# A recommender tower on one core: rows stored chunk by chunk, half loads in long runs, and GpSimd's index add moved to the head of its chunk

## The chip, the cores and the metric

The kernel runs on one core of a Trainium2 chip. The time is the device time of one execution in microseconds. Before the change it was 2475.34 us, the median of three runs from 2474.52 to 2476.03.

## The reference, cut to what matters

39 embedding tables are read at 2048 x 39 ids (rows of D = 16 floats). Three layers then each form all products of a field of the input with a field of the layer before, weigh them with W and sum, per sample b and embedding position d. A small dense part of two hidden layers ends it.

```python
e = stack([tbl_f[ids[:, f]] for f in range(39)], axis=1)        # (2048, 39, 16)
x0 = xk = e
for idx, (W, b) in enumerate([(w0, b0), (w1, b1), (w2, b2)]):
    z = relu(einsum('bhd,bkd,hks->bsd', x0, xk, W) + b[None, :, None])
    if idx != 2:
        xk = z[:, :64, :];  direct.append(z[:, 64:, :])
    else:
        direct.append(z)
logit = sum(concatenate(direct, axis=1), axis=-1)                # (2048, 256)
h = concatenate([logit, dense_ctx], axis=1)
h = maximum(h @ W_top1 + b_top1, 0);  h = maximum(h @ W_top2 + b_top2, 0)
y = h @ W_top3
```

All of it is float32. W is (39, 39, 128) in layer 0 and (39, 64, 128) in layers 1 and 2.

## The kernel before, in words

The 2048 samples are done in 64 chunks of CB = 32, so a tile's free size is CN = 32 x 16 = 512. A chunk c has three stages, one per layer, and every engine does them in the order stage 1 of c, stage 0 of c + 1, stage 2 of c.

**Rows.** GpSimd gathers a chunk's rows three chunks ahead: it adds each table's first row to the ids (`index`, L417) and issues ten indirect DMAs (L429) into `rows_sb[p]`, p being the chunk's parity. SP stores these rows transposed to a DRAM tensor `x0_rows` (L336, six DMAs of 64-byte pieces). `x0_rows` has one line of all 2048 samples per field (58 lines, fields 0 to 18 a second time after the 39), so a chunk's piece of a field is 2 KB and neighbouring fields of a chunk lie 128 KB apart. From it the operands are loaded:

- `xa`, `xb` (L346, L350): for stage 0, three blocks of 39 partitions each, the fields and the shifted fields, all issued by SP.
- `xh[p]` (L304): for stages 1 and 2, every field spread over 64 partitions. Tile t holds field 2t in partitions 0 to 63 (SP's DMA) and field 2t + 1 in partitions 64 to 127 (ScalarE's DMA). There are 20 tiles and 39 fields; the last tile's upper half is cleared at the start (`pads_cleared`), by a memset of GpSimd for each of the two buffers.

**Products.** VectorE multiplies two tiles at once, 128 x 1024 (L516). A pair (a "group") has one of three kinds. WHOLE goes to TensorE as float32. The other two are split in a rounded high part, made by ScalarE (L775), and the rest, the low part, made by GpSimd (L458, BY_POOL) or by VectorE (L490, BY_DVE). A split tile takes three fast matmuls, a whole tile two slow ones of two passes each (L627). Per chunk GpSimd makes ten low parts: four in stage 1, two in stage 0, four in stage 2. In a chunk that gathers, one indirect DMA follows each low part; chunk 0 issues twenty, for chunks 2 and 3, and chunks 61 to 63 issue none.

**What sets the order around the change.** Each engine has its own instruction stream, written out by hand in the blocks `sync`, `gpsimd`, `vector`, `tensor`, `scalar`; the engines meet at semaphores. Chunks 0 and 1 and the last two (four on GpSimd) are written out, the others are a loop of two chunks a turn, with waits on register values. In GpSimd's `chunk`, `begin_gather` comes after the chunk's first low part: it waits for the ids, adds, waits for `stored[p]` (the rows buffer is free once the chunk before in it is stored) and for its own add. SP's `chunk(c)` stores the rows of c, fetches the ids of c + 2, waits for its stores, loads `xa` and `xb`, then the lower half of `xh`, and stores the sums of chunk c - 2. ScalarE issues the upper half of chunk c + 1 at the head of its chunk c. After the 64 chunks the dense part runs, in buffers that are free by then.

Of the kernel before, what the change touches and what calls it, by code (L numbers as in the profile page):

```python
# [44 lines left out]
G0, GK = -(-T0 // PAIR), TK // PAIR  # L45
# [3 lines left out]
KINDS = {  # L49
    0: [BY_POOL, BY_DVE, BY_POOL, WHOLE],  # L50
    1: [WHOLE, BY_POOL, WHOLE, BY_DVE, BY_POOL, WHOLE, BY_POOL, BY_DVE, BY_POOL, WHOLE],
}
KINDS[2] = KINDS[1]
# [18 lines left out]
class Group:  # L72


    def __init__(self, stage, chunk, g, counts):
        total = T0 if stage == 0 else TK
        self.stage, self.chunk, self.g, self.kind = stage, chunk, g, KINDS[stage][g]
        self.tiles = range(PAIR * g, min(PAIR * (g + 1), total))
        self.ends_layer = self.tiles[-1] == total - 1
        self.rows = 128 if stage else (LAST0 if self.ends_layer else JT * F)  # L80
# [11 lines left out]
def plan():  # L92


    counts = dict.fromkeys(("all", "split", WHOLE, BY_POOL, BY_DVE), 0)
    order = [(0, 0)]
    for c in range(CHUNKS):
        order += [(1, c)] + [(0, c + 1)] * (c + 1 < CHUNKS) + [(2, c)]
    return {(stage, c): [Group(stage, c, g, counts) for g in range(len(KINDS[stage]))]
            for stage, c in order}  # L100
# [5 lines left out]
WHOLES = [g for g in EVERY if not g.split]  # L106
LIKE = 2

PER = {"all": sum(map(len, KINDS.values())),
       "split": sum(k != WHOLE for ks in KINDS.values() for k in ks),  # L110
       BY_POOL: sum(k == BY_POOL for ks in KINDS.values() for k in ks),
       BY_DVE: sum(k == BY_DVE for ks in KINDS.values() for k in ks)}
assert (PER["all"] - PER["split"]) % WHOLE_SLOTS == 0
assert PER[BY_POOL] % POOL_SLOTS == 0 and PER["split"] % SPLIT_SLOTS == 0
# [10 lines left out]
def tower(nc, table, ids, row_base, ctx_t, staged, wt1, wt1c, wt2, cols, out):  # L125
# [3 lines left out]
    x0_dram = nc.dram_tensor("x0_rows", (XROWS, N), f32, kind="Internal").ap()  # L129
    feats_dram = nc.dram_tensor("feats_all", (128, 2, B), f32, kind="Internal").ap()  # L130

    with ExitStack() as stack:
# [60 lines left out]

        def split_places(weights, products):
# [16 lines left out]
        wt2_end = -(-(3 * T1 + n1 * T2) // S)  # L211
        WT2_FREE = 1 + max(g.n for g in PLAN[2, CHUNKS - 1]
                           if g.split and SPLIT_TILE[2, g.tiles[0]] < wt2_end)
        INPUTS_FREE = 1 + max(g.n for g in SPLITS if g.split_slot < 2)
# [17 lines left out]
        pads_cleared = sem("pads_cleared")  # L232
# [33 lines left out]
        def groups(stage, c):  # L266

            return PLAN[stage, c if isinstance(c, int) else LIKE + (stage == 0)]

        def count(c, group, value, per):  # L270


            if isinstance(c, int):
                return value
            return (c - group.chunk) * PER[per] + value
# [10 lines left out]
        def over_chunks(engine, step, tail=2):  # L286

            step(0, 0)
            step(1, 1)
            with engine.Fori(1, (CHUNKS - tail) // 2) as i:  # L290
                step(2 * i, 0)
                step(2 * i + 1, 1)
            for c in range(CHUNKS - tail, CHUNKS):
                step(c, c % 2)
# [12 lines left out]
        N_GROUPS, N_SPLIT = len(firsts), sum(g.split for g in firsts)  # L307
# [11 lines left out]
        def _(sp):  # L319
            def load_ids(c, p):  # L320
                sp.dma_start(ids_sb[p][:, :], ids[bass.ds(c * 128, 128), :]).then_inc(ids_loaded[p], 16)

            def store_rows(c, p):

                sp.wait_ge(gathered[p], 8 * GATHERS * (c - p) + 16 * GATHERS)
                col = x0_dram[:, bass.ds(c * CN, CN)]
                for again in range(2):
                    for g in range(FG):  # L330
                        f0 = g * GATHERS
                        n = min(GATHERS, (XROWS - F if again else F) - f0)
                        if n > 0:
                            src = rows_sb[p][g * CB:(g + 1) * CB, 0:n * D]
                            dst = col[again * F + f0:again * F + f0 + n, :]
                            sp.dma_start(dst.rearrange("f (b d) -> b f d", d=D),  # L336
                                         src.rearrange("b (f d) -> b f d", d=D)
                                         ).then_inc(stored[p], 16)

            def load_pairs(c):  # L340

                col = x0_dram[:, bass.ds(c * CN, CN)]
                for jj in range(JT):
                    n = (SHIFTS - jj + JT - 1) // JT
                    at = slice(jj * F, (jj + 1) * F)
                    sp.dma_start(xa[at, :], col[0:F, :]).then_inc(x0_loaded, 16)  # L346
                    step = col.ap[0][0]
                    shifted = bass.AP(tensor=col.tensor, offset=col.offset + jj * step,
                                      ap=[[step, F], [JT * step, n], [1, CN]])
                    sp.dma_start(xb[at, 0:n, :], shifted).then_inc(x0_loaded, 16)  # L350

            def store_feats(c, p):

                sp.wait_ge(direct_summed, c + 1)
                sp.wait_ge(last_summed, c + 1)
# [56 lines left out]
        def _(pool):  # L412
# [65 lines left out]
            for g in groups(0, 0):  # L478
                if g.kind == BY_POOL:
                    low_parts(g, 0)  # L480
# [461 lines left out]
```

## Time and profile before

| what | value |
|---|---|
| profiled execution's own time | 2474.38 us |
| its span | 2472.6 us |
| TensorE busy | 2373.9 us, 96% |
| VectorE busy | 2212.4 us, 89% |
| GpSimd busy | 2155.9 us, 87% |
| ScalarE busy | 1364.1 us, 55% |
| DMA moved | 467 MB, 189 GB/s over the span |

Busy is the sum of an engine's instructions; matmuls overlap and their ends are modelled, so TensorE's share is not its share of peak. Register instructions and the issue of plain DMAs are not counted as busy; an indirect DMA on GpSimd is. An engine's idle time is put down to the semaphore that ended it, or to "issue" when nothing that the profile shows was waited for.

### The profile page before, as it was taken

The page shows a single profiled execution, that of the slowest core. Times are in us where ns is not written, and L with a number is a line of the kernel's source. Part 1 is how long each engine was busy: PE and PEld are TensorE (multiplying, and loading weights), DVE is VectorE, ACT ScalarE, POOL GpSimd, SP SyncE. Part 2 cuts the span into 40 slices and gives each one's busy share as a digit, 9 for nine tenths or more (in the row PEclk, how much of TensorE's full clock was granted, in tenths as well). Part 3 has the DMA queues.
Part 4 walks back from the last instruction along what each step waited for, and adds up shares of the span by engine and source line. Part 5 has one row for each costly group of instructions (what it writes and reads, how often), then busy time and mean ns, then how long its engine had stood idle before and what let it go on. Part 6 is the DMA issues. An engine that isn't in the chain of part 4 may idle for free. (4 is left out here: it accounts for less than half of the span.)

```text
span 2472.6 us, 32417 instructions
## 1 busy us (share of the span) xinstructions
PE 2373.9 (96%) x8192; PEld 1539.6 (62%) x8192; DVE 2212.4 (89%) x2047; ACT 1364.1 (55%) x1532; POOL 2155.9 (87%) x1350
## 2 busy tenths in 40 slices
PE   1799999999999999999999999999999999999999
PEld 1466666666666666666666666666666666666665
DVE  2689999999999999999999999999999999999983
ACT  2355555555555555555555555555555555555552
POOL 4799999999999999999999999999999999999640
PEclk9899999999999999999999999999999999999999
DMA  7888888888878888888888788888888878888710
GB/s 179 187 187 207 196 185 211 212 173 209 207 186 194 210 209 176 204 211 181 203 204 209 177 204 212 181 206 205 201 180 208 214 177 208 208 188 191 199 55 1
DMA packets 398547, 467.04 MB, mean 189 GB/s; under 512 B 170337, under 2 KB 179553, under 8 KB 398257
## 3 DMA queue, kind: packets, MB, share of 16 engines
q1 hardware_dynamic: 299202, 302.30, 54.3%
q10 hardware_dynamic: 78848, 159.39, 24.7%
q0 software_dynamic: 20480, 5.15, 1.8%
q8 instruction: 8, 0.13, 0.0%
q14 instruction: 9, 0.07, 0.0%
HBM read 457.03 MB, written 9.71 MB: 189 GB/s over the span
## 5 line engine op out<-in xcount | busy, mean ns | idle before, releaser
L458 POOL TENSOR_TENSOR low<-prod_pool,high 128x1024 fp32r<-128x1024 f32 (+1 forms) x640 | 1532.5, 2395 | 88.8 <-ACT high L775 73.2
L775 ACT ACTIVATE high<-prod_pool 128x1024 fp32r<-128x1024 f32 (+1 forms) x640 | 677.3, 1058 | 733.5 <-DVE prod_pool L516 695.9
L627 PE MATMUL z<-prod_whole,w_whole 128*128 128x512 f32 (+1 forms) x2176 | 1011.5, 594 | 5.6 <-DVE prod_whole L516 5.6
L627 PE MATMUL z<-high,w_high 128*128 128x512 f32 (+1 forms) x1920 | 939.5, 489 | 55.9 <-ACT high L775 55.9
L627 PE MATMUL z<-high,w_low 128*128 128x512 f32 (+1 forms) x1920 | 758.6, 395 | 0.0
L429 POOL DMA_INDIRECT rows<-table,index x640 | 611.5, 955 | 147.8 <-issue 99.0
L516 DVE TENSOR_TENSOR prod_whole<-xh,x 128x1024 f32<-128x1024 f32 x512 | 620.5, 1212 | 110.1 <-PE z L627 90.8
L627 PE MATMUL z<-low,w_high 128*128 128x512 f32 (+1 forms) x1920 | 614.0, 401 | 33.5 <-POOL low L458 33.3
L627 PEld LDWEIGHTS z<-prod_whole,w_whole 128*128 128x128 f32 (+1 forms) x2176 | 412.7, 190 | 355.7 <-issue 296.8
L516 DVE TENSOR_TENSOR prod_pool<-xh,x 128x1024 f32<-128x1024 f32 x512 | 621.3, 1213 | 10.0 <-POOL low L458 10.0
L627 PEld LDWEIGHTS z<-high,w_high 128*128 128x128 f32 (+1 forms) x1920 | 363.6, 189 | 229.2 <-issue 141.1
L627 PEld LDWEIGHTS z<-high,w_low 128*128 128x128 f32 (+1 forms) x1920 | 363.8, 189 | 172.4 <-issue 107.5
L627 PEld LDWEIGHTS z<-low,w_high 128*128 128x128 f32 (+1 forms) x1920 | 356.3, 189 | 145.2 <-POOL low L458 66.3
L775 ACT ACTIVATE high<-prod_dve 128x1024 fp32r<-128x1024 f32 (+1 forms) x320 | 328.5, 1026 | 170.2 <-DVE prod_dve L516 154.9
L490 DVE TENSOR_TENSOR low<-prod_dve,high 128x1024 fp32r<-128x1024 f32 (+1 forms) x320 | 391.3, 1223 | 3.3
L516 DVE TENSOR_TENSOR prod_dve<-xh,x 128x1024 f32<-128x1024 f32 x256 | 312.8, 1222 | 0.0
L516 DVE TENSOR_TENSOR prod_pool<-xb,xa_ps 117x1024 f32<-117x1024 f32 x128 | 155.6, 1215 | 79.6 <-POOL low L458 40.6
L752 ACT ACTIVATE x<-z,cols_sb 64x512 f32<-64x512 f32 x256 | 166.6, 651 | 63.0 <-PE z L627 44.5
L757 ACT ACTIVATE direct<-z,cols_sb 64x512 f32<-64x512 f32 x128 | 87.5, 684 | 33.9 <-DVE chunk_feats L528 32.3
L516 DVE TENSOR_TENSOR prod_dve<-xb,xa_ps 117x1024 f32<-117x1024 f32 x64 | 78.2, 1221 | 0.0
L765 ACT ACTIVATE xa_ps<-xa 117x512 f32<-117x512 f32 x64 | 38.6, 603 | 43.0 <-DMA xb<-x_rows 41.5
L742 ACT ACTIVATE last<-z,cols_sb 128x512 f32<-128x512 f32 x64 | 42.7, 668 | 4.9 <-PE z L627 4.9
(45 smaller groups left out, 365.5 us busy)
## 6 DMA issues: line engine op xcount, KB each, us to landing
xh<-x_rows SPq DMA_DIRECT2D x64, 2560.0 KB, 16.5
xh<-x_rows ACTq DMA_DIRECT2D x64, 2432.0 KB, 20.6
xb<-x_rows SPq DMA_DIRECT2D x128, 546.0 KB
xb<-x_rows SPq DMA_DIRECT2D x64, 468.0 KB
xa<-x_rows SPq DMA_DIRECT2D x192, 78.0 KB
rows<-table,index POOLq DMA_INDIRECT x640
x_rows<-rows SPq DMA_DIRECT2D x256, 20.0 KB
xh<-staged SPq DMA_DIRECT2D x2, 1280.0 KB, 6.9
```

Of the source, the lines that this page charges most:

```text
L429: pool.indirect_dma_start(rows_sb[p][0:n, j * D:(j + 1) * D], None, table, bass.IndirectOffsetOnAxis(ap=index[p][0:n, j:j + 1], axis=0),). ...
L458: pool.tensor_tensor(low[0:g.rows, g.split_slot, 0:n, :], prod_pool[0:g.rows, g.slot, 0:n, :], high[0:g.rows, g.split_slot, 0:n, :].bitcas ...
L490: dve.tensor_tensor(low[0:g.rows, g.split_slot, 0:n, :], prod_dve_v[0:g.rows, 0:n, :], high[0:g.rows, g.split_slot, 0:n, :].bitcast(f32), ...
L516: dve.tensor_tensor(into[0:g.rows, 0:n, :], spread[0:g.rows, t, :], shared[0:g.rows, :].unsqueeze(1).broadcast_to([g.rows, n, CN]), ALU.mu ...
L627: return pe.matmul(z[stage][:, :], weights[0:g.rows, table[stage, t], :], src[0:g.rows, i, :], start=t == 0 and weights is not w_low and s ...
L742: act.activation(last[:, :], z[2][:, :], ACT.Relu, bias=bias[2]).then_inc(relu_done[2], 1)
L752: act.activation(xk[stage][half, :], z[stage][feed, :], ACT.Relu, bias=bias[stage][feed, :]).then_inc(relu_done[stage], 1)
L757: act.activation(direct[leave, :], z[stage][leave, :], ACT.Relu, bias=bias[stage][leave, :]).then_inc(relu_done[stage], 1)
L765: act.activation(xa_ps[0:JT * F, :], xa[:, :], ACT.Copy).then_inc(xa_copied, 1)
L775: act.activation(high[0:g.rows, g.split_slot, 0:n, :], src[0:g.rows, 0:n, :], ACT.Copy).then_inc(high_ready, 1)
```

## The change

The order of fields in memory, the packets of the `xh` loads and the place of one small instruction change.

- `x0_rows` becomes (64 x 58) lines of 512, a chunk's 58 fields one after the other (`rows_of`).
- Tile t of `xh` holds fields t and 20 + t. The lower half of a chunk is one run of 40 KB per partition, the upper half one of 38 KB (`load_run`), cut by `max_dma_last_dim`. The last tile's upper half gets field 19 again, by a third DMA, and its weights are zero (`by_fields`), so the two memsets and `pads_cleared` go.
- GpSimd's `begin_gather` is parted. `make_index` (both waits and the add) comes ahead of the chunk's first low part, `begin_gather` keeps the wait for the add. In chunk 0 this holds for the first of its two gathers.
- In the dense part the split parts of the context lie in the weights' buffers instead of the products', and h1's two places further front.
- A class `Chunk` carries a chunk's number and parity, and the list of groups names each group's first tile; the groups are the same.

GpSimd's stream, in the loop, from the last gather of a chunk to the first of the next. `low` are the low parts, `rows` the gathered rows. Before:

```order
L458 TENSOR_TENSOR low<-prod_pool,high 128x1024 [waits high_ready]
L429 DMA rows1<-table,index1 96x16
L279 ISA
L458 TENSOR_TENSOR low<-prod_pool,high 128x1024 [waits high_ready]
L416 ISA
L417 TENSOR_TENSOR index0<-ids0,row_base_sb 128x10 [waits ids_loaded0]
L421 REGISTER_ALU
L422 REGISTER_ALU [waits stored0]
L429 DMA rows0<-table,index0 128x16 [waits index_ready]
```

The same place in the changed kernel:

```order
L481 TENSOR_TENSOR low<-prod_pool,high 128x1024 [waits high_ready]
L451 DMA rows1<-table,index1 96x16
L436 ISA
L439 REGISTER_ALU [waits ids_loaded0]
L440 TENSOR_TENSOR index0<-ids0,row_base_sb 128x10 [waits stored0]
L303 REGISTER_ALU
L481 TENSOR_TENSOR low<-prod_pool,high 128x1024 [waits high_ready]
L444 REGISTER_ALU
L451 DMA rows0<-table,index0 128x16 [waits index_ready]
```

The add and its two waits moved from behind the chunk's first low part to ahead of it; the gather's wait for the add stayed where it was.

SP's stream, in the loop, the loads of one chunk. Before:

```order
L279 ISA [waits stored0]
L346 DMA xa<-x0_rows 39x512 [waits products_ready]
L350 DMA xb<-x0_rows 39x7x512
L350 DMA xb<-x0_rows 39x6x512
L279 REGISTER_ALU
L304 DMA xh0<-x0_rows 64x20x512 [waits products_ready]
```

In the changed kernel:

```order
L303 ISA [waits stored0]
L371 DMA xa<-x0_rows 39x512 [waits products_ready]
L374 DMA xb<-x0_rows 39x7x512
L374 DMA xb<-x0_rows 39x6x512
L303 REGISTER_ALU
L330 DMA xh0<-x0_rows 64x5x2048 [waits products_ready]
L330 ISA
L330 DMA xh0<-x0_rows 64x512
```

SP's one load of twenty runs of 512 floats per partition became one of five runs of 2048 and a short one. ScalarE's load at the same place went from 19 runs of 512 to 8 runs of 1216 floats.

The diff, cut to its core (the many lines where only `c, p` became `c` are left out):

```diff
+RUN_BYTES = 4 * CN * 4
+HALF_TILE = TK - 1
...
-    x0_dram = nc.dram_tensor("x0_rows", (XROWS, N), f32, kind="Internal").ap()
+    x0_dram = nc.dram_tensor("x0_rows", (CHUNKS * XROWS, CN), f32, kind="Internal").ap()
...
-                    "feats": [x[:, 0:2, :], x[:, 3:5, :]],
-                    "ctx": [x[0:CTX, 2, :], x[0:CTX, 5, :]],
-                    "h1": x[:, 6:6 + n1, :]}
+                    "feats": [x[:, 0:2, :], x[:, 2:4, :]],
+                    "ctx": [w[0:CTX, CTX_AT:CTX_AT + MB], w[0:CTX, CTX_AT + MB:CTX_AT + 2 * MB]],
+                    "h1": x[:, 4:4 + n1, :]}
...
-        def load_fields(engine, c, p, hh):
-
-            col = x0_dram[:, bass.ds(c * CN, CN)]
-            step = col.ap[0][0]
-            n = (F + 1 - hh) // 2
-            spread = bass.AP(tensor=col.tensor, offset=col.offset + hh * step,
-                             ap=[[0, H], [2 * step, n], [1, CN]])
-            engine.dma_start(xh[p][hh * H:(hh + 1) * H, 0:n, :], spread).then_inc(xh_loaded[p], 16)
+        def rows_of(c):
+
+            return x0_dram[bass.ds(c.n * XROWS, XROWS), :]
+
+        def load_run(engine, c, part, tiles, field):
+
+            of = rows_of(c)
+            n = len(tiles)
+            spread = bass.AP(tensor=of.tensor, offset=of.offset + field * CN,
+                             ap=[[0, H], [1, n * CN]])
+            into = xh[c.p][part * H:(part + 1) * H, tiles[0]:tiles[0] + n, :]
+            engine.dma_start(into.rearrange("p t n -> p (t n)"), spread,
+                             max_dma_last_dim=RUN_BYTES).then_inc(xh_loaded[c.p], 16)
...
-                load_fields(sp, c, p, 0)
+                load_run(sp, c, 0, range(0, TK), 0)
+                load_run(sp, c, 1, range(HALF_TILE, TK), HALF_TILE)
...
-            def begin_gather(c, p):
-
-
-                pool.wait_ge(ids_loaded[p], 8 * (c - p) + 16)
-                pool.tensor_tensor(index[p][:, :], ids_sb[p][:, :], row_base_sb[:, :],
+            def make_index(c):
+                pool.wait_ge(ids_loaded[c.p], 8 * (c.n - c.p) + 16)
+                if not c.known or c.n >= 2:
+
+                    pool.wait_ge(stored[c.p], 8 * STORES * (c.n - c.p))
+                pool.tensor_tensor(index[c.p][:, :], ids_sb[c.p][:, :], row_base_sb[:, :],
                                    ALU.add).then_inc(index_ready, 1)
-                if not isinstance(c, int) or c >= 2:
-
-                    pool.wait_ge(stored[p], 8 * STORES * (c - p))
-                pool.wait_ge(index_ready, c + 1)
+
+            def begin_gather(c):
+                pool.wait_ge(index_ready, c.n + 1)
...
+                if ahead:
+                    make_index(ahead[0])
                 for i, (g, at) in enumerate(mine):
                     low_parts(g, at)
                     for _ in range(-(-len(left) // (len(mine) - i))):
-                        at, q, j = left.pop(0)
+                        at, j = left.pop(0)
                         if j == 0:
-                            begin_gather(at, q)
-                        gather(q, j)
+                            if at is not ahead[0]:
+                                make_index(at)
+                            begin_gather(at)
+                        gather(at.p, j)
...
-                dve.wait_ge(xh_loaded[p], 16 * (c - p) + 32)
+                dve.wait_ge(xh_loaded[c.p], 24 * (c.n - c.p) + 48)
...
-                load_fields(act, c, p, 1)
+                load_run(act, c, 1, range(0, HALF_TILE), TK)
...
-        tiles = np.zeros((2 * TK, H, w.shape[2]), w.dtype)
-        tiles[:F] = w
-        return np.ascontiguousarray(tiles.reshape(TK, 2 * H, w.shape[2]).transpose(1, 0, 2))
+        upper = np.concatenate([w[TK:], np.zeros_like(w[HALF_TILE:TK])])
+        return np.ascontiguousarray(np.concatenate([w[:TK], upper], axis=1).transpose(1, 0, 2))
```

## Rows read from the trace of the kernel before

**Rows 1.** The page's head.

```profile
span 2472.6 us, 32417 instructions
```

**Rows 2.** By stretch: busy of PE, PEld, DVE, ACT, POOL; clock; DMA share; GB/s.

```profile
1300.00:1600.00 300.00, 296.80 (x1029) 193.13 (x1028) 282.34 (x259) 173.51 (x192) 279.31 (x175) 1.00 0.85 196
```

**Rows 3.** Waits of PE, 100 to 2400 us: us in total, times, longest.

```profile
PE z L627 <- POOL low L458: 29.2, 64, 1.7
```

**Rows 4.** Timeline of PE: start, us, operation [idle before <-releaser].

```profile
1225.76 0.72 PE L627 MATMUL z<-low,w_high 117*128 117x512 f32 x2 [0.37 <-POOL low L458]
```

**Rows 5.** Groups on POOL, 200 to 2200 us: busy, mean ns | idle before.

```profile
L458 POOL TENSOR_TENSOR low<-prod_pool,high 128x1024 fp32r<-128x1024 f32 (+1 forms) x553 | 1324.7, 2396 | 14.9 <-ACT high L775 0.7
L429 POOL DMA_INDIRECT rows<-table,index x553 | 528.3, 955 | 123.9 <-issue 79.3 <-POOL index L417 44.6
```

**Rows 6.** Waits of POOL, 200 to 2200 us.

```profile
POOL rows L429 <- POOL index L417: 44.6, 55, 0.8
POOL low L458 <- ACT high L775: 0.7, 4, 0.2
```

**Rows 7.** Timeline of POOL over a chunk's edge.

```profile
1237.43 2.41 POOL L458 TENSOR_TENSOR low<-prod_pool,high 128x1024 fp32r<-128x1024 f32 x1
1239.99 0.92 POOL L429 DMA_INDIRECT rows<-table,index  x1 [0.16 <-issue]
1241.05 2.36 POOL L458 TENSOR_TENSOR low<-prod_pool,high 128x1024 fp32r<-128x1024 f32 x1
1243.38 0.21 POOL L417 TENSOR_TENSOR index<-ids,row_base_sb 128x10 int32<-128x10 int32 x1
1244.40 0.97 POOL L429 DMA_INDIRECT rows<-table,index  x1 [0.82 <-POOL index L417]
1245.39 2.40 POOL L458 TENSOR_TENSOR low<-prod_pool,high 128x1024 fp32r<-128x1024 f32 x1
```

**Rows 8.** Timeline of POOL at the start, before any low part.

```profile
15.78 0.92 POOL L429 DMA_INDIRECT rows<-table,index  x1 [0.30 <-issue]
16.73 0.29 POOL L417 TENSOR_TENSOR index<-ids,row_base_sb 128x10 int32<-128x10 int32 x1
```

**Rows 9.** Timeline of POOL in the last chunks, which gather nothing.

```profile
2312.19 2.38 POOL L458 TENSOR_TENSOR low<-prod_pool,high 128x1024 fp32r<-128x1024 f32 x1 [3.80 <-ACT high L775]
...
2347.62 2.37 POOL L458 TENSOR_TENSOR low<-prod_pool,high 128x1024 fp32r<-128x1024 f32 x1 [3.25 <-ACT high L775]
```

**Rows 10.** Timeline of SP, one chunk.

```profile
1216.79 2.98 SPq L336 DMA_DIRECT2D x_rows<-rows  x6
1219.99 1.22 SPq L321 DMA_DIRECT2D ids<-ids  x1
1223.67 0.35 SPq L346 DMA_DIRECT2D xa<-x_rows  x1
```

**Rows 11.** Timeline of ACT in chunks 0 and 1.

```profile
44.83 0.60 ACT L765 ACTIVATE xa_ps<-xa 117x512 f32<-117x512 f32 x1 [28.20 <-DMA xb<-x_rows]
...
83.44 0.60 ACT L765 ACTIVATE xa_ps<-xa 117x512 f32<-117x512 f32 x1 [13.31 <-DMA xb<-x_rows]
```

**Rows 12.** Timeline of PE in chunk 0.

```profile
85.07 0.79 PE L627 MATMUL z<-high,w_high 128*128 128x512 f32 x1 [7.89 <-ACT high L775]
```

**Rows 13.** By stretch: chunk 0's loads; the pairs' loads alone.

```profile
22.00:44.80 22.80, 0.00 (x0) 0.00 (x0) 0.00 (x0) 0.00 (x0) 6.71 (x8) 1.00 1.02 201
...
1223.00:1236.00 13.00, 12.63 (x44) 7.94 (x43) 12.83 (x12) 7.28 (x9) 12.45 (x8) 1.00 0.73 144
```

**Rows 14.** The page's DMA issues: KB each, median us to landing.

```profile
xh<-x_rows ACTq DMA_DIRECT2D x64, 2432.0 KB, 20.6
xb<-x_rows SPq DMA_DIRECT2D x128, 546.0 KB
xb<-x_rows SPq DMA_DIRECT2D x64, 468.0 KB
xa<-x_rows SPq DMA_DIRECT2D x192, 78.0 KB
```

**Rows 15.** DMA queues (q1 SP, q10 ACT), 1208 to 1214 us: packets, MB, share.

```profile
q1 hardware_dynamic: 541, 1.11, 52.5%
q10 hardware_dynamic: 532, 1.09, 51.5%
```

More of the change, by code:

```diff
@@ L75, in __init__ @@
     def __init__(self, stage, chunk, g, counts):
[L76 to L80, printed above, removed]
+        of = GROUPS[stage]
+        self.stage, self.chunk, self.g = stage, chunk, g
+        self.kind, first, n = of[g]
+        self.tiles = range(first, first + n)
+        self.begins_layer, self.ends_layer = g == 0, g == len(of) - 1
+        self.rows = 128 if stage else (LAST0 if first == T0 - 1 else JT * F)
         self.split = self.kind != WHOLE
@@ L98, in plan @@
         order += [(1, c)] + [(0, c + 1)] * (c + 1 < CHUNKS) + [(2, c)]
-    return {(stage, c): [Group(stage, c, g, counts) for g in range(len(KINDS[stage]))]
+    return {(stage, c): [Group(stage, c, g, counts) for g in range(len(GROUPS[stage]))]
             for stage, c in order}
@@ L107, with __init__, __add__, __sub__ @@
 LIKE = 2
[L109 to L114, printed above, removed]
+ALL_KINDS = [kind for groups in GROUPS.values() for kind, _, _ in groups]
+PER = {"all": len(ALL_KINDS), "split": sum(k != WHOLE for k in ALL_KINDS),
+       BY_POOL: ALL_KINDS.count(BY_POOL), BY_DVE: ALL_KINDS.count(BY_DVE)}
+assert 2 * (PER["all"] - PER["split"]) % WHOLE_SLOTS == 0
+assert 2 * PER[BY_POOL] % POOL_SLOTS == 0 and 2 * PER["split"] % SPLIT_SLOTS == 0
+class Chunk:
+    def __init__(self, n, like):
+        self.n, self.like = n, like
+        self.known = isinstance(n, int)
+        self.p = like % 2
+    def __add__(self, k):
+        if self.known:
+            return Chunk(self.n + k, self.n + k)
+        return Chunk(self.n + k, LIKE + (self.like + k) % 2)
+    def __sub__(self, k):
+        return self + -k
 WHOLE_TILE, SPLIT_TILE = {}, {}
@@ L266, in groups @@
         def groups(stage, c):
-            return PLAN[stage, c if isinstance(c, int) else LIKE + (stage == 0)]
+            return PLAN[stage, c.like]
         def count(c, group, value, per):
-            if isinstance(c, int):
+            if c.known:
                 return value
-            return (c - group.chunk) * PER[per] + value
+            return (c.n - group.chunk) * PER[per] + value
         def wait_count(engine, semaphore, c, group, value, per):
@@ L432, in gather, with chunk @@
                 ).then_inc(gathered[p], 16)
-            def chunk(c, p):
-                known = isinstance(c, int)
-                gathers = [(c + 3, 1 - p)] if not known or c + 3 < CHUNKS else []
-                if known and c == 0:
-                    gathers.insert(0, (2, 0))
-                left = [(at, q, j) for at, q in gathers for j in range(GATHERS)]
+            def chunk(c):
+                ahead = [c + 3] if not c.known or c.n + 3 < CHUNKS else []
+                if c.known and c.n == 0:
+                    ahead.insert(0, c + 2)
+                left = [(at, j) for at in ahead for j in range(GATHERS)]
                 stages = [(1, c), (0, c + 1), (2, c)]
-                if known and c == CHUNKS - 1:
+                if c.known and c.n == CHUNKS - 1:
                     stages.pop(1)
                 mine = [(g, at) for s, at in stages for g in groups(s, at) if g.kind == BY_POOL]
+                if ahead:
+                    make_index(ahead[0])
                 for i, (g, at) in enumerate(mine):
@@ L639, in contract @@
                         for i in every:
[L640 removed]
+                            done = mm(w_whole, WHOLE_TILE, src, i, i == 0, i == every[-1])
                     else:
@@ L646, in contract, with chunk @@
                         for i in every:
-                            mm(w_high, SPLIT_TILE, highs, i)
+                            mm(w_high, SPLIT_TILE, highs, i, i == 0)
                             mm(w_low, SPLIT_TILE, highs, i)
-                        made = low_by_pool if g.kind == BY_POOL else low_by_dve
                         wait_count(pe, made, c, g, g.of_kind + 1, g.kind)
                         for i in every:
-                            done = mm(w_high, SPLIT_TILE, lows, i, i == every[-1])
+                            done = mm(w_high, SPLIT_TILE, lows, i, last=i == every[-1])
                     done.then_inc(products_used, 1)
-            def chunk(c, p):
+            def chunk(c):
                 contract(1, c)
-                if not (isinstance(c, int) and c == CHUNKS - 1):
+                if not (c.known and c.n == CHUNKS - 1):
                     contract(0, c + 1)
@@ L760, in copy_xa @@
             def copy_xa(c):
-                act.wait_ge(x0_loaded, (c + 1) * 2 * JT * 16)
-                if not (isinstance(c, int) and c == 0):
+                act.wait_ge(x0_loaded, (c.n + 1) * 2 * JT * 16)
+                if not (c.known and c.n == 0):
                     wait_made(act, 0, c - 1)
```

215 lines of the change are left out of this document (105 added, 110 removed).

## The prediction, made before the result was known

> **What bounds the kernel now.** I began with the busy times of a steady stretch, since the span of 2472.6 us [rows 1] is almost all one repeated chunk. In 300 us of it TensorE is busy 296.8 us, VectorE 282.3, GpSimd 279.3 [rows 2]. By that view TensorE is the bound and GpSimd has 7% to spare. The second view, what TensorE waited for, says otherwise: 64 waits, one per chunk, 29.2 us in all, every one for a low part made by GpSimd [rows 3]. In the timeline such a wait stands in stage 0, before the last split group: 0.37 us of idle time by the page's modelled ends [rows 4].
>
> So the third view is GpSimd's own. Between 200 and 2200 us its low parts and gathers are busy 1324.7 + 528.3 us, and the idle time just before them is 14.9 + 123.9 us [rows 5]. That is 1991.8 of 2000 us; the small index adds fill the rest. Of that idle time 44.6 us in 55 pieces is put down to the index add, and a low part waits for nobody worth naming [rows 5, 6]. An engine whose gaps are all its own and that waits for no other engine is the bound, whatever its busy share says. GpSimd does 553 low parts in those 2000 us, ten to a chunk, so a chunk takes 2000 / 55.3 = 36.17 us.
>
> What would the next bound be? The last three chunks gather nothing, and there GpSimd waits for ScalarE. The same low part of two neighbouring chunks starts at 2312.19 and 2347.62 [rows 9]: 35.43 us. That is the chunk with GpSimd out of the way, TensorE's pace. So at most 36.17 - 35.43 = 0.74 us per chunk can be won in the steady part.
>
> **The index add.** In a gathering chunk GpSimd does low part, index add, gather, and then nine times low part, gather. In a normal step a low part follows the gather's end by 0.02 us and the gather follows the low part's end by 0.16 us. At the index add it is different [rows 7]: the low part ends at 1241.05 + 2.36 = 1243.41, the gather starts at 1244.40, that is 0.99 us instead of 0.16. So the index add costs 0.83 us there, 0.2 us of work of which most runs into the low part's tail, and 0.82 us of waiting between it and the gather that reads it.
>
> After the change the add stands ahead of the chunk's first low part, and the gather's wait for it comes 2.4 us of low part later. The wait is then long met, and the gather should follow the low part by 0.16 us like the others. The 0.83 us go. What comes is the add itself between the last gather of one chunk and the first low part of the next. This gap is 1241.05 - (1239.99 + 0.92) = 0.14 us now [rows 7]. Without register work an add starts 0.03 us after a gather's end and takes 0.29 us (15.78 + 0.92 = 16.70 against 16.73) [rows 8]; in the loop one more register instruction stands ahead of it. I put the new cost at 0.1 us for that instruction plus the 0.21 us of the add in the loop [rows 7]: 0.31, rounded up to 0.33 us. The net gain is 0.83 - 0.33 = 0.50 us per chunk, and the chunk becomes 35.67 us, still GpSimd's pace, with TensorE waiting 0.24 instead of 0.74 us.
>
> The bounds: the add could hide entirely (0.83, of which TensorE lets only 0.74 through), or bring its 0.21 us and a gap like that of 0.82 us [rows 7] to its new place, which loses 0.20: -0.20 to 0.74. I take 0.50, since the low part does not read the index and so has no such gap to wait out.
>
> It counts in chunks 1 to 60, the ones that gather one later chunk: 60 x 0.50 = 30 us. In chunk 0 GpSimd gathers twice and otherwise waits for ScalarE, and I count nothing.
>
> The moved add also carries two waits, for the ids and for the stores of the chunk two before, and behind it now stand all of GpSimd's low parts, which TensorE needs. SP issues those stores at 1216.79 and goes on past its own wait for them at 1223.67 [rows 10]; the add would stand at 1241, 17 us later. So the waits are met.
>
> **The transfers.** The lower half's load becomes five runs of 8192 bytes per partition instead of twenty of 2048, ScalarE's load of the upper half eight runs of 4864 bytes, and a third load brings field 19 once more into the upper half of the last tile: 64 x 2 KB = 131 KB and one more issue on SP. In the steady part I count all this at nothing. What hides it is time: the pairs' loads are issued from 1223.67 on [rows 10] and nobody waits for them after the first two chunks. If that cover went, each us of lateness would be a us of the chunk.
>
> At the start it is not hidden. ScalarE waits 28.20 us for the pairs of chunk 0 and 13.31 us for those of chunk 1 [rows 11], and the second costs TensorE 7.89 us [rows 12]. While chunk 0's pairs load, from 22 to 44.8 us, ScalarE's half xh load runs beside them; the core moves 201 GB/s [rows 13]. The pairs are 2 x 546 + 468 + 3 x 78 = 1794 KB, the half 2432 KB [rows 14]: 4226 KB, 21.0 us at that rate. The bounds for the two chunks together: at the rate at which two halves land at once (1.11 + 1.09 MB in 6 us, 367 GB/s) [rows 15] chunk 0's loads would take 4226 / 367 = 11.5 us, 11 us less, and chunk 1's whole 7.89 us would go: -19. If ScalarE's longer packets went first and the pairs came alone after them at 144 GB/s [rows 13], 2432 / 201 + 1794 / 144 = 24.6 us, 2 us more for each chunk: +4. I take -2, near the row of 201 GB/s, which is this very pair of loads.
>
> By the packet counts the two queues take turns packet by packet: 541 against 532 packets in 6 us where both load halves [rows 15]. The Trainium skill says the same (DMA: Bandwidth & Descriptors, Queues, rings and completion order): each DMA engine goes round its queues and changes at packet boundaries. That rule speaks against the change: with 4864-byte packets on ScalarE's queue and 2048-byte ones on SP's, the pairs would get 30% of the rate instead of half. By it ScalarE's half would take 2432 / 141 = 17.2 us, the pairs would have 1040 KB by then and 754 KB more at 144 GB/s: 22.4 us, no gain. With equal shares it would be 2 x 1794 / 201 = 17.9 us. The -2 lies between.
>
> The Trainium skill also says (DMA: Bandwidth & Descriptors, Latency and other measured facts) that copies of rows a large power of two apart in HBM are slower, 207 against 214 GB/s at the smallest pitch it gives. This change takes the pitch from 128 KB to 2 KB; by that figure it would be an estimated 3% of 22 us, 0.7 us, inside the term above.
>
> The rest is worth nothing: the cleared pads ran while GpSimd waited for a load or after its gathers, the context's split parts only move within the last phase, and TensorE's, VectorE's and ScalarE's arithmetic is the same in number and shape.
>
> **The sum.** The profiled execution took 2474.38 us, 1.8 more than its span and 1.0 less than the median of the runs. 2474.4 - 30 - 2 = 2442.4; against the median it would be 2443.3. I say 2443.
>
> **Rivals.** (A) The add hides and TensorE becomes the bound: 60 x 0.74 = 44 us, 2474.4 - 44 - 2 = 2428. For it: the add ran into the low part's tail in the loop [rows 7]. Against it: a gather seems to hold GpSimd's instruction stream, since even a low part comes 0.14 us late at the chunk's edge.
>
> (B) The start gains much, since its 201 GB/s are half of what the core moves elsewhere [rows 13, 15]: -19 instead of -2, 2425. Against it: the pairs go to 39 partitions at a time and load at 144 GB/s even alone, and their runs stay at 2 KB.
>
> (C) The wait only moves: the first low part waits out the 0.82 us behind the add: 2474.4 - 2 = 2472. Against it: no operand in common.
>
> (D) Slower: GpSimd now waits for the stores and ids with its low parts behind it. Should the longer packets hold up SP's 64-byte stores, the add's place decides: the stores land by 1223.67 and are needed at 1241, so from 17 us of delay on each further us is one of the chunk; with 1 us it is 60 x 1 = 60 us, less the 30 won: 2504. Before, one low part was let through first. Against it: a whole half of xh lands 20.6 us after its issue today [rows 14], so 17 us is the length of a whole load, not of some longer packets.
>
> **How the numbers follow.** My forecast has 0.62, A 0.18, B 0.10, C 0.05, D 0.05. Runs of this kernel spread over 1.5 us, so under 0.2%, 5 us, I call it no change. Faster: forecast, A and B, 0.90; same: C, 0.05; slower: D, 0.05. The forecast's own range is 2433 to 2455 (0.35 to 0.65 us per chunk, start -2 to +2). The range for 8 in 10 takes in A and B and, upwards, an add that saves only 0.25 us per chunk: 2424 to 2459.
>
> **What would show it.** In the changed trace: no gather waits for the index add, which costs 45 us of idle time now; an add of 0.2 us stands between a gather and a low part, and the low part follows it at once; ten low parts take 35.6 to 35.8 us; TensorE's wait for low parts falls to about a third but stays (to nothing in case A). ScalarE's two waits for the pairs stay near 28 and 13 us. I am wrong if low parts keep a period of 36.2 us, if a low part waits for the add, or if the add waits for a DMA.

## The result: slower, and the profile after

The changed kernel takes 2491.02 us (median of 7 runs, 2481.18 to 2503.74), the kernel before 2475.34 (2473.32 to 2476.03) on the same chip: a ratio of 1.0068 with a 95% interval of 1.0044 to 1.0092. The forecast was 2443 in a range of 2424 to 2459. The profiled execution took the median's 2491.02 us; the page's head, beside [rows 1]:

```profile
span 2489.2 us, 32602 instructions
```

At the chunk's edge the index add did what was forecast. The timeline of POOL over a chunk's edge, to set beside [rows 7]:

```profile
1612.10 0.92 POOL L451 DMA_INDIRECT rows<-table,index  x1 [0.16 <-issue]
1613.04 0.22 POOL L440 TENSOR_TENSOR index<-ids,row_base_sb 128x10 int32<-128x10 int32 x1
1613.40 2.37 POOL L481 TENSOR_TENSOR low<-prod_pool,high 128x1024 fp32r<-128x1024 f32 x1
1615.92 0.97 POOL L451 DMA_INDIRECT rows<-table,index  x1
```

The gather that follows the add's low part starts 1615.92 - 1615.77 = 0.15 us after it; it was 0.99. The low part starts 1613.40 - 1613.02 = 0.38 us after the last gather; it was 0.14. Nothing waits for the index any more, as the waits of POOL, 200 to 2200 us, say (us in total, times, longest), beside [rows 6]:

```profile
POOL rows L451 <- issue: 72.1, 456, 0.2
POOL low L481 <- ACT high L786: 44.1, 54, 4.9
```

The second row is the new trouble. Before, four low parts waited 0.7 us for ScalarE; now 54 wait 44.1 us. And yet in the same 2000 us GpSimd does three low parts fewer than in [rows 5], 550 for 553 (groups on POOL):

```profile
L481 POOL TENSOR_TENSOR low<-prod_pool,high 128x1024 fp32r<-128x1024 f32 (+1 forms) x550 | 1318.0, 2396 | 58.5 <-ACT high L786 44.1
```

So the mean chunk went from 36.17 to 2000 / 55.0 = 36.36 us instead of to the 35.67 that were forecast. TensorE's wait for low parts is hardly shorter than in [rows 3], and a wait for ScalarE has come (waits of PE, 100 to 2400 us):

```profile
PE z L640 <- POOL low L481: 27.1, 49, 1.7
PE z L640 <- ACT high L786: 6.3, 5, 1.9
```

What does ScalarE wait for? The waits of ACT, 200 to 2200 us:

```profile
ACT high L786 <- DVE prod_pool L531: 551.6, 297, 2.5
ACT high L786 <- DVE prod_dve L531: 112.7, 93, 1.2
ACT xa_ps L776 <- DMA xb<-x_rows: 53.4, 21, 6.0
```

The third row does not exist before: there the copy of xa waited for the pairs at the start alone [rows 11]. Now it does so in 21 of 55 chunks. The other end of the thread is SP. Its waits over the same 2000 us, before and then after:

```profile
SPq L355 <- DVE chunk_feats L528: 801.6, 56, 14.4
SPq L304 <- DVE prod_whole L516: 520.0, 55, 10.8
```

```profile
SPq L378 <- DVE chunk_feats L543: 794.8, 55, 18.4
SPq L330 <- DVE prod_whole L531: 73.9, 47, 4.3
```

Before it loads its half of xh, SP waits for VectorE to be done with the old half. That wait is harmless; it is SP's slack. It was 520.0 / 55 = 9.5 us per chunk and is 73.9 / 55 = 1.3. One late chunk in full, on SP's, ScalarE's and ScalarE's DMA queue:

```profile
1933.28 0.35 SPq L371 DMA_DIRECT2D xa<-x_rows  x1
...
1936.29 1.35 SPq L330 DMA_DIRECT2D xh<-x_rows  x2
1936.36 0.63 ACTq L330 DMA_DIRECT2D xh<-x_rows  x1
1953.28 0.60 ACT L776 ACTIVATE xa_ps<-xa 117x512 f32<-117x512 f32 x1 [5.96 <-DMA xb<-x_rows]
...
1957.20 9.83 SPq L362 DMA_DIRECT2D x_rows<-rows  x6
...
1969.68 0.35 SPq L371 DMA_DIRECT2D xa<-x_rows  x1
```

The pairs are issued at 1933.28 and both halves of xh right behind them; the last xb lands 20 us later, when ScalarE has stood for 5.96 us. Issuing the six stores holds SP for 9.83 us; before it was 2.98 [rows 10], and SP's half came 13.3 us after the pairs, just as these landed (13.7 us after their issue in the mean). 33.3 us pass from the upper half's issue to the next pairs' issue. Before it was 22.8 (rows of ScalarE's DMA queue and of SP):

```profile
1236.98 0.65 SPq L304 DMA_DIRECT2D xh<-x_rows  x1
1238.24 0.62 ACTq L304 DMA_DIRECT2D xh<-x_rows  x1
...
1261.01 0.35 SPq L346 DMA_DIRECT2D xa<-x_rows  x1
```

At the start ScalarE's two waits for the pairs are 32.72 and 12.86 us, 28.20 and 13.31 before [rows 11]:

```profile
49.26 0.60 ACT L776 ACTIVATE xa_ps<-xa 117x512 f32<-117x512 f32 x1 [32.72 <-DMA xb<-x_rows]
...
86.98 0.60 ACT L776 ACTIVATE xa_ps<-xa 117x512 f32<-117x512 f32 x1 [12.86 <-DMA xb<-x_rows]
```

### The profile page after: what moved, and what is told of

It reads as the page before. It is cut to its first block, busy times and chain, and to the rows that moved or that the text cites. A ratio compares the mean times of both kernels' runs of the same rounds, so it can differ in the third digit from the quotient of the medians.

```text
span 2489.2 us, 32602 instructions
## 1 busy us (share of the span) xinstructions
PE 2380.5 (96%) x8192; PEld 1535.6 (62%) x8192; DVE 2210.2 (89%) x2047; ACT 1364.6 (55%) x1532; POOL 2160.9 (87%) x1348
## 4 chain that ended last, share of the span: by engine, by line
POOL 65%; issue 16%; PE 13%; DMA 3%; SPq 2%; ACT 1%; DVE 1%; POOLq 1%; ACTq 0%; DVEq 0%
POOL low L481 45%; POOL rows L451 19%; PE z L640 10%; DMA xb<-x_rows 2%; SPq L362 1%; DMA x_rows<-rows 1%; POOL index L440 0%; DMA rows<-table,index 0%; ACT high L786 0%; PE x L712 0%; DVE prod_pool L531 0%; PE z L731 0%; PE prod_dve L712 0%; PE z L733 0%; POOLq L303 0%
## 5 line engine op out<-in xcount | busy, mean ns | idle before, releaser
L543 DVE TENSOR_REDUCE chunk_feats<-last 128x32 f32<-128x512 f32 x64 | 43.6, 681 | 58.1 <-ACT last L753 58.1
```

Of the source, the lines that this page charges most:

```text
L543: dve.tensor_reduce(into, src[:, :].rearrange("p (b d) -> p b d", d=D), axis=AX.X, op=ALU.add).then_inc(done, 1)
```

## The experiments

In the table, xb is the steady wait of ScalarE's copy for the pairs, and slack SP's wait before its half of xh, both over 200 to 2200 us (total, times). These two come from the one execution that was profiled; for e4 it took 2498.20 us, 13 more than its median. The ratio is to the kernel before, on the same chip as the run.

| kernel | us | ratio, 95% interval | xb | slack |
|---|---|---|---|---|
| before | 2475.34 | 1 | none | 520.0, 55 |
| the change | 2491.02 | 1.0068 [1.0044, 1.0092] | 53.4, 21 | 73.9, 47 |
| e1 index add only | 2451.01 | 0.9902 [0.9885, 0.9918] | none | 510.4, 56 |
| e2 change in 2 KB runs | 2452.22 | 0.9906 [0.9889, 0.9922] | none | 476.2, 56 |
| e3 change, add in its old place | 2499.33 | 1.0104 [1.0087, 1.0121] | 29.9, 14 | 98.6, 52 |
| e4 equal halves, 8 KB | 2484.95 | 1.0035 [1.0012, 1.0059] | 56.5, 17 | 118.0, 52 |
| e5 lower half long, upper 2 KB | 2558.94 | 1.0345 [1.0325, 1.0365] | 132.7, 41 | 25.3, 16 |
| e6 lower half 2 KB, upper long | 2454.51 | 0.9915 [0.9899, 0.9932] | none | 449.3, 56 |
| e7 equal halves, 2 KB | 2451.87 | 0.9903 [0.9887, 0.9920] | none | 476.8, 56 |
| e8 equal halves, 4 KB | 2454.13 | 0.9914 [0.9897, 0.9930] | none | 371.5, 56 |
| e9 change, fewer pairs | 2452.98 | 0.9913 [0.9896, 0.9929] | none | 288.8, 56 |
| e10 e7 + 1.3 MB | 2454.98 | 0.9921 [0.9905, 0.9938] | none | 475.4, 56 |
| e11 e7 + 2.6 MB | 2459.01 | 0.9937 [0.9917, 0.9957] | none | 168.0, 55 |
| e12 e7 + 5.2 MB | 3464.65 | 1.3999 [1.3976, 1.4022] | 576.4, 39 | none |

The figure of e11 is the median of three executions; a fourth took 2539.29 us and was not traced, so what made it long is open.

**Which part of the change is it?** e1 is the kernel before with the add moved; e2 the whole change with runs of 2 KB; e3 the change without the moved add; e4 the change without the third load, both halves being one run of 20 tiles.

```diff
 e1, in before's chunk()
+                if gathers:
+                    make_index(*gathers[0])
 e2
-RUN_BYTES = 4 * CN * 4
+RUN_BYTES = CN * 4
 e3, in chunk()
-                if ahead:
-                    make_index(ahead[0])
...
-                            if at is not ahead[0]:
-                                make_index(at)
+                            make_index(at)
 e4
-                load_run(sp, c, 1, range(HALF_TILE, TK), HALF_TILE)
-                load_run(act, c, 1, range(0, HALF_TILE), TK)
+                load_run(act, c, 1, range(0, TK), TK)
```

> The kernel before with GpSimd's index add alone moved; memory order and loads as before. If the predicted mechanism holds and the loss comes from the loads (theories T and L): chunks of 35.6 to 35.7 us, no long ones, 2440 to 2447 us. If the moved add itself causes the long chunks (rival I, its two waits now stand ahead of all low parts): about 2490 us with scattered long chunks.

> The changed kernel with its xh loads cut into runs of 2048 bytes instead of 8192 and 4864; chunk-major rows, third load and index add as in the changed kernel. Theory T (long packets take the turns of the pairs' 2 KB packets and slow the two halves): ScalarE's waits for xb in the steady part vanish (53 us now), halves land at about 395 GB/s again, 2438 to 2450 us. Theory L (the new order in memory or the extra load is what makes the loads slow): still 2480 to 2500 us with waits for xb.

> The changed kernel with the index add back behind the chunk's first low part. T and L: the loads' loss stays and the index add's gain goes; the long chunks take a little less away since the pace is 36.2 instead of 35.6 us and so the pairs have 0.5 us more: 2500 to 2520 us. Rival I: 2475 us, no long chunks.

> The changed kernel with the upper half as one run of 20 tiles like the lower (field 0's second copy fills the last tile, weights zero): both in 8192-byte packets, no third load. T: turns of 8192 against 2048 bytes take still more from the pairs, so as slow as the changed kernel or slower, 2490 to 2520 us. If the third load or the odd 4864-byte packets were the cause: 2440 to 2450 us.

e1 and e2 gain 24 and 23 us; e3 loses 24, e4 10. The forecasts had the directions right, but each figure lies just outside its range: e1 by 4 us, e2 by 2, e3 by 1, e4 by 5. The chunk-major rows, the third load and the other pairing of fields stand in e2 too and cost nothing there that can be told from e1. The add gains wherever it is alone. The loss comes with the long packets, and with nothing else that was changed.

e1 also shows what the add is worth. Its chunk's edge (timeline of POOL), to set beside [rows 7], and its groups on POOL, 200 to 2200 us:

```profile
1194.23 0.92 POOL L429 DMA_INDIRECT rows<-table,index  x1 [0.16 <-issue]
1195.16 0.23 POOL L418 TENSOR_TENSOR index<-ids,row_base_sb 128x10 int32<-128x10 int32 x1
1195.48 2.37 POOL L462 TENSOR_TENSOR low<-prod_pool,high 128x1024 fp32r<-128x1024 f32 x1
1197.99 0.98 POOL L429 DMA_INDIRECT rows<-table,index  x1
```

```profile
L462 POOL TENSOR_TENSOR low<-prod_pool,high 128x1024 fp32r<-128x1024 f32 (+1 forms) x559 | 1340.8, 2399 | 23.4 <-ACT high L780 11.1
```

A chunk takes 2000 / 55.9 = 35.78 us, 0.39 less than before. At the edge the gap ahead of the gather fell from 0.99 to 0.14 us and the gap ahead of the low part rose from 0.14 to 0.33: 0.85 us went and 0.19 came, so 0.66 could have been had. Part of the rest is a new wait, once per chunk, at the start of stage 2 (timelines of POOL, ACT and DVE):

```profile
1216.91 2.37 POOL L462 TENSOR_TENSOR low<-prod_pool,high 128x1024 fp32r<-128x1024 f32 x1 [0.21 <-ACT high L780]
```

```profile
1211.94 1.33 ACT L757 ACTIVATE x<-z,cols_sb 64x512 f32<-64x512 f32 x2 [1.05 <-PE z L632]
...
1215.78 1.06 ACT L780 ACTIVATE high<-prod_pool 128x1024 fp32r<-128x1024 f32 x1 [1.80 <-DVE prod_pool L521]
```

```profile
1213.39 1.23 DVE L521 TENSOR_TENSOR prod_whole<-xh,x 128x1024 f32<-128x1024 f32 x1 [1.80 <-PE z L632]
1214.53 1.21 DVE L521 TENSOR_TENSOR prod_pool<-xh,x 128x1024 f32<-128x1024 f32 x1
```

Followed back, this low part waits for ScalarE's high part, that for VectorE's product, and VectorE and ScalarE for TensorE's end of stage 1. GpSimd has caught up with TensorE. Between 200 and 2200 us of e1 the trace shows no wait of TensorE at all. By stretch, before and then e1 (busy of PE, PEld, DVE, ACT, POOL; clock; DMA share; GB/s):

```profile
200.00:2200.00 2000.00, 1977.70 (x6857) 1287.62 (x6856) 1876.51 (x1713) 1149.92 (x1273) 1861.26 (x1161) 1.00 0.85 199
```

```profile
200.00:2200.00 2000.00, 1998.26 (x6933) 1301.19 (x6931) 1894.64 (x1734) 1163.52 (x1288) 1888.41 (x1174) 1.00 0.86 201
```

TensorE's own work is the same in both, 1977.70 / 55.3 = 35.76 and 1998.26 / 55.9 = 35.75 us per chunk. So before the change only 36.17 - 35.76 = 0.41 us per chunk stood idle on it, and the add could win no more than that.

**Which long packets?** In e5 only the lower half (SP) keeps its 8 KB runs, in e6 only the upper half (ScalarE) its 4864-byte ones.

```diff
-                             max_dma_last_dim=RUN_BYTES).then_inc(xh_loaded[c.p], 16)
 e5
+                             max_dma_last_dim=CN * 4 if part else RUN_BYTES).then_inc(xh_loaded[c.p], 16)
 e6
+                             max_dma_last_dim=RUN_BYTES if part else CN * 4).then_inc(xh_loaded[c.p], 16)
```

> The changed kernel with SP's lower half in runs of 8192 bytes and ScalarE's upper half in runs of 2048. Theory T1 (long packets lower the rate at which the two halves land together, and everything behind them on SP's queue comes late): both mixed kernels lose about half of it, 2460 to 2480 us, this one the more since its packets are longer. Theory T2 (only ScalarE's long packets hurt, by taking the turns of the pairs' 2 KB packets on SP's queue): this one is as fast as with short runs, 2450 to 2455 us.

> The changed kernel with SP's lower half in runs of 2048 bytes and ScalarE's upper half in its eight runs of 4864. T1: 2455 to 2475 us, less slow than lower_long. T2: as slow as the changed kernel, about 2490 us, with ScalarE waiting some 50 us for xb in the steady part.

I had held it possible that ScalarE's long packets do the harm by taking the pairs' turns. That fell: e6 loses nothing, and e5 is the slowest of the six. Theory T1 kept its direction for e5, not its size: e5 lies 79 us above the range that it gave. e6 lies 0.5 us below its own. So the loss hangs on SP's 8 KB half; ScalarE's 4864-byte half alone costs no time. The DMA queues of e5 (q1 SP, q10 ScalarE; packets, MB, share of 16 engines) at 1025 to 1031 us, where both halves load, and at 1038 to 1044:

```profile
DMA packets 388, 1.57 MB, mean 261 GB/s; under 512 B 52, under 2 KB 80, under 8 KB 239
...
q1 hardware_dynamic: 155, 1.22, 79.9%
q10 hardware_dynamic: 157, 0.32, 22.1%
```

```profile
DMA packets 1451, 1.23 MB, mean 204 GB/s; under 512 B 863, under 2 KB 890, under 8 KB 1451
...
q10 hardware_dynamic: 532, 1.08, 85.0%
q1 hardware_dynamic: 857, 0.13, 19.6%
```

155 packets against 157: by these counts the queues take turns packet by packet, so the upper half gets a fifth of the rate (0.32 of 1.57 MB). It is left over when the lower half is done and drags on beside the stores. In e6 it is SP's half that falls behind, at 343 against 346 packets:

```profile
DMA packets 753, 2.39 MB, mean 299 GB/s; under 512 B 32, under 2 KB 64, under 8 KB 753
...
q10 hardware_dynamic: 343, 1.67, 68.8%
q1 hardware_dynamic: 346, 0.71, 33.5%
```

**How long is too long?** e7 and e8 are e4 with runs of 2 and of 4 KB.

```diff
-RUN_BYTES = 4 * CN * 4
+RUN_BYTES = CN * 4        # e7
+RUN_BYTES = 2 * CN * 4    # e8
```

> Both halves one run of 20 tiles in chunk-major rows, cut into 2048 bytes, no third load, index add moved. T1 and T2: no long packets, so as short_runs, 2448 to 2453 us; 131 KB per chunk and one issue less change nothing, being hidden. If the third load cost something: 2445 us or less.

> The same in runs of 4096 bytes, twice the packet. T1: the rate of the two halves together falls between 275 and 395 GB/s, 2453 to 2470 us. T2: turns of 4096 against 2048 bytes give the pairs a third, 2455 to 2475 us. If only packets near 8 KB do harm: 2450 us.

Neither loses time, but SP's slack falls from 8.5 to 6.6 us per chunk with 4 KB runs, and with 8 KB (e4) to 2.1. Slack shrinks in steps, while time is lost only where it nears nothing. So I formed the theory that the transfers of a chunk close a loop: the pairs, both halves, the stores, and then the next chunk's pairs, which SP issues only when the stores have landed. By it nothing is lost until this loop has used up the room that a chunk leaves it.

**Is it the loop or the packets?** e9 leaves the long packets alone and takes other bytes out of the loop; e10 to e12 put bytes into it, all in 2 KB packets.

```diff
 e9, in load_pairs()
-                    n = (SHIFTS - jj + JT - 1) // JT
+                    n = (SHIFTS - jj + JT - 1) // JT if c.known else 3
 e10 (SPARE = 10), e11 (SPARE = 20), e12 (SPARE = 20, twice), behind SP's half
+                of = rows_of(c)
+                src = bass.AP(tensor=of.tensor, offset=of.offset,
+                              ap=[[0, H], [1, SPARE * CN]])
+                sp.dma_start(spare_dram[bass.ds(c.n * H, H), :], src,
+                             max_dma_last_dim=RUN_BYTES).then_inc(spared, 16)
```

> The changed kernel with its long packets untouched, but from chunk 2 on only 9 of the 20 tiles of xb are loaded per chunk (878 KB of 1794 KB of pairs stay away; the rest of xb keeps old data, so the sums differ). Theory (the transfers of one chunk, pairs, both halves, six stores, run one behind the other in a loop that SP and its queue close, and the long packets stretch that loop from about 26 us to the chunk's own length): the pairs shrink by 878 KB at about 131 KB/us, 6.7 us, and the loop gets its slack back: no steady wait of xa_ps for xb, about 2452 us (2449 to 2458), SP waits again some 5 to 7 us per chunk before its half. Rival (8 KB packets do harm by themselves, by delaying whatever other packet is under way, however much is to be moved): part of the 53 us wait of xa_ps stays and the time stays above 2465 us.

> All runs of 2 KB (the kernel with equal halves in 2 KB packets, 2451.9 us), and behind SP's half one more transfer per chunk on its queue, 10 x 2 KB x 64 = 1311 KB from x_rows to a spare tensor in HBM that nobody reads. Theory of the loop: at 205 KB/us, the rate of one half alone, that is 6.4 us more in the loop, and SP has 476.8 / 56 = 8.5 us of slack before its half: hidden, 2450 to 2456 us, no steady wait for xb, SP's wait down to some 1 to 3 us per chunk. Rival (only long packets hurt): also 2452, with the slack unchanged at 8 us.

> As the run before, with 20 x 2 KB x 64 = 2621 KB of spare transfer per chunk. Theory of the loop: 12.8 us more against 8.5 us of slack: 4.3 us too much per chunk if all of it came at that rate, and since two thirds of the transfers run beside each other in a full loop at some more, I expect 1 to 4.3 us per chunk x 59 chunks: 2510 to 2705 us, the same waits of xa_ps for xb as in the changed kernel and more of them, and a full SP without a wait before its half, all in 2 KB packets. Rival (only long packets hurt): 2452 us, no steady wait for xb.

> The kernel with equal halves in 2 KB packets and two spare transfers of 2621 KB per chunk on SP's queue, from HBM to HBM. Measured so far: with one of them SP's wait before its half fell from 8.5 us to 168.0 / 55 = 3.1 us per chunk, 5.4 us for one, and nothing was lost in the steady part. Theory of the loop: two cost 10.8 us, 2.3 us more than the slack of 8.5, so the chunk grows from 35.8 to about 38 us: 59 x 2.3 = 136 us, 2590 us (2500 to 2680, as the second may load at another rate), ScalarE's copy waits for xb in most chunks and SP no longer waits before its half, without one packet over 2 KB. Rival (only long packets hurt): no wait for xb, about 2460 us.

e9 came as the loop has it: with all its 8 KB packets the kernel comes within 2 us of e1, has no steady wait for xb, and SP has 288.8 / 56 = 5.2 us of slack; the rival had put it above 2465 us. (The 878 KB count 1000 bytes each; in the unit of the 1794 KB they are 858.) e10 lost nothing, but its slack did not fall either, 475.4 us against e7's 476.8, where the theory had left 1 to 3 us per chunk; its halves and stores take 23.3 us like e7's. That is what the rival had said, and why is not shown. e11 missed: the spare transfer, from HBM to HBM, moves at 410 GB/s (1004 to 1006 us), twice what I had assumed, and 3.1 us of slack stayed. e12 overfilled the loop, and the wait that came with the long packets is there without one of them; the rival's 2460 us fell. The waits of its ACT, 200 to 2200 us, and SP's two spare issues in one chunk:

```profile
ACT xa_ps L786 <- DMA xb<-x_rows: 576.4, 39, 15.7
```

```profile
1019.19 28.73 SPq L410 DMA_DIRECT2D spare<-x_rows  x2
```

That is 14.8 us per chunk, and its chunk takes 52 us. The direction was the loop's, the size was not: I had put 38. With the slack gone the pairs run beside the halves and take 23.6 us (table below), and the spare issues hold SP itself for 28.73 us. So e12 shows that a full loop costs time without long packets; how much a full loop of this kernel costs it does not show.

The loop can be read from the issues and landings of the traces (means of the chunks between 300 and 2150 us): from ScalarE's issue of the upper half to the issue of the next pairs, which wait for the stores, and from there to the pairs' landing.

| us | before | e1 | e7 | e6 | e8 | e11 | e9 | e3 | e4 | the change | e5 | e12 |
|---|---|---|---|---|---|---|---|---|---|---|---|---|
| halves and stores | 22.7 | 22.6 | 23.3 | 23.8 | 25.2 | 28.8 | 26.7 | 30.7 | 30.6 | 31.2 | 34.2 | 52.0 |
| pairs | 13.7 | 13.6 | 13.5 | 13.6 | 13.7 | 13.8 | 7.5 | 15.1 | 15.9 | 15.7 | 16.5 | 23.6 |
| sum | 36.4 | 36.2 | 36.8 | 37.4 | 38.9 | 42.6 | 34.2 | 45.8 | 46.5 | 46.9 | 50.7 | 75.6 |

Undisturbed, ScalarE copies xa 11.0 us after its issue of an upper half, one chunk on: 35.8 + 11.0 = 46.8 us after the one in the table (e1). Kernels whose sum is 4 us or more below that lose nothing in the steady part. The change and e4 stand at it in the mean, e3 1.4 us below its own 36.2 + 11.0 = 47.2, so that some chunks are late and others not; e5 and e12 are beyond. The times say the same: at the edge they scatter, from 2472.48 to 2502.43 us in e4 and from 2481.18 to 2503.74 with the change, while e1 stays within 2450.63 to 2451.90.

## Why the prediction was wrong

- **The index add: right in kind, too large in size.** The gather's wait went, and the waits for ids and stores were met. "0.31, rounded up to 0.33 us" for the add in its new place is what e1 shows between the last gather and the low part (1195.48 against the gather's end at 1195.15; the changed kernel 0.38). But that is the whole gap, and the sum did not credit the 0.14 us that had stood there. With it the edge gives 0.66 us instead of 0.50, and yet e1 won 0.39 per chunk, 24 us and not 30. What the sum had wrong is TensorE's pace. The 35.43 us of [rows 9] are a chunk that gathers nothing; in the chunks that gather, TensorE has 35.76 us of work. The prediction's own [rows 3], 29.2 / 64 = 0.46 us per chunk, already said that no 0.50 could come through. Why TensorE works 0.3 us longer in those chunks is open.
- **The transfers: the step that failed.** "In the steady part I count all this at nothing. What hides it is time: the pairs' loads are issued from 1223.67 on [rows 10] and nobody waits for them after the first two chunks." That nobody waits showed that there was cover, not how much. The cover was 10.6 us (46.8 - 36.2 in e1), and the change took it whole: 8.6 us more for halves and stores, 2.1 more for the pairs. It cost the 24 us that the add had won and some 16 more. The sentence "each us of lateness would be a us of the chunk" was somewhat high: 53.4 us of waits for xb in 2000 us make some 57 in 59 chunks, against 40 us between the changed kernel and e1.
- **The rate.** The prediction read 367 GB/s for two halves from 2 KB packets [rows 15], used it for a bound of the start, and nowhere asked what two halves in the changed lengths would move. They moved 285. It held the two queues' turns against the pairs at the start alone, not against the two halves and the stores behind them.
- **The start:** -2 us was forecast; the two waits for the pairs grew from 41.5 us together to 45.6. In e1, whose loads are those of before, they are 44.2, in e9, whose first two chunks load as the change's do, 44.0, and over all runs they lie between 40.5 (e5) and 46.4 (e4). So most of the growth is scatter, and no gain is seen. (The prediction's sums for the start divide KB of 1024 bytes by GB/s of 10^9 and come out 2% short; nothing hangs on it.)
- **Rival D** was the nearest. Long packets do hold up SP's stores, and I gave it 0.05. But it looked for the price at the add, which had 17 us of room; the price was paid at the pairs behind those stores, which had 10.6. A's time did not come, but its mechanism did in e1, where TensorE is the bound, at 35.78 us and not at 35.43. B did not come; C is excluded by the low part's 0.38 us.

## What to carry to other kernels

A transfer that nobody waits for has a slack that can be read: add up the chain from its release over the queue it stands in to its use, here 36.2 of 46.8 us (e1), and hold the change's extra time against the rest. A wait of a DMA-issuing engine that looks like waste can be such slack, as SP's 9.5 us per chunk before its half of xh were here. Longer packets are not a free gain: with two queues busy, look at what both move together and at who shares turns with the long packets. And what a change can win at one engine is held against what the next one stands idle in the same stretch, not in another.

## What the runs showed of the hardware

One half of xh alone, 64 partitions, loads at the same rate in 2 KB packets (e2's upper half, 1029 to 1032 us) and in 8 KB packets (e9's lower half, 1016 to 1020 us):

```profile
DMA packets 298, 0.61 MB, mean 203 GB/s; under 512 B 0, under 2 KB 0, under 8 KB 298
```

```profile
DMA packets 99, 0.81 MB, mean 203 GB/s; under 512 B 0, under 2 KB 0, under 8 KB 0
```

Two halves on two queues move almost twice that in 2 KB packets (e2, 1022 to 1026 us) and in 4 KB packets (e8, 1024 to 1028), but not in 8 KB packets (e4, 1002 to 1012), nor in the change's 8 KB and 4864 B (1954 to 1962):

```profile
DMA packets 822, 1.57 MB, mean 393 GB/s; under 512 B 46, under 2 KB 62, under 8 KB 822
```

```profile
DMA packets 438, 1.55 MB, mean 387 GB/s; under 512 B 48, under 2 KB 64, under 8 KB 438
```

```profile
DMA packets 423, 2.68 MB, mean 268 GB/s; under 512 B 67, under 2 KB 99, under 8 KB 99
```

```profile
DMA packets 488, 2.28 MB, mean 285 GB/s; under 512 B 104, under 2 KB 121, under 8 KB 334
```

So short packets of the two halves overlap almost fully, 8 KB packets only in part. Mixed lengths fall too: 299 GB/s with 4864 bytes beside 2 KB (e6, above) and 261 with 8 KB beside 2 KB (e5). Why is not shown by any run here, nor where between 4096 and 8192 bytes the rate of two equal lengths falls. The Trainium skill (DMA: Bandwidth & Descriptors, SWDGE vs HWDGE vs iDMA) prefers packets of at most 4096 bytes, in its account of the descriptors that GpSimd builds; on SP's and ScalarE's queues the 387 GB/s of e8 and the 268 of e4 agree. It also says (SBUF — State Buffer, "Can I just issue two DMAs to hit both halves?") that two transfers at once, one to each half of the partitions, gain only 6% over one; 393 against 203 GB/s disagree, and the measurement decides.

The distance of the rows in HBM made no difference that can be told: 128 KB in e1, 2 KB in e7, 2451.0 and 2451.9 us. The times alone could hide one, since both kernels have room for it; but the pairs also take 13.6 and 13.5 us to land.

In e12, where TensorE stands idle a quarter of the time, the granted clock is 0.87 in the mean, against 1.00 in the steady part of the kernel before [rows 2]. By stretch (busy of PE, PEld, DVE, ACT, POOL; clock; DMA share; GB/s), one chunk of e12:

```profile
1015.00:1067.00 52.00, 39.78 (x127) 24.65 (x126) 34.79 (x33) 20.67 (x23) 33.74 (x22) 0.87 0.99 242
```
